# An edge-loop step of a graph attention layer: one VectorE product of 1024 columns instead of two of 512, and first-column additions at other places

## The chip, the cores and the metric

One core of one Trainium2 chip runs the kernel. The metric is the device time of one execution in microseconds (us), as the median of several runs. The engines are TensorE (PE in the profile; PEld is its weight load), VectorE (DVE), ScalarE (ACT), GpSimd (POOL) and SyncE (SP). Each works through its own queue in order; semaphores make one wait for another, or for its own earlier instruction.

## The reference

Relation-aware graph attention, a residual and a layer norm, in float32. N = 6250 nodes of 256 features, E = 100000 edges sorted by destination, 5 relations, 4 heads of 64.

```python
Q = (einsum('nc,rch->rnh', x, Wq) + bq[:, None, :]).reshape(R, N, HEADS, OUT)   # K, V alike
q_i = Q[edge_type, dst];  k_j = K[edge_type, src];  v_j = V[edge_type, src]
score = sum(q_i * k_j, axis=-1) * scale
seg = dst * R + edge_type
m = segment_max(score, seg);  e = exp(score - m[seg]);  s = segment_sum(e, seg)
alpha = e / s[seg]
out = segment_sum(v_j * alpha[..., None], dst).reshape(N, HD) + bias
x = layernorm(x + out, axis=-1)
```

## The kernel before

**Stages.** First the edges are sorted by segment on VectorE (a sorting network) while TensorE projects x to Q, K and V, which go to tables in HBM. Then comes the edge loop, which is what this document is about, and then a short stage that joins chunk borders, adds bias and x, and normalizes.

**The edge loop.** The edges stand in 831 tiles of 128, four tiles to a step, so 208 steps (`NSB`), and eight steps (`PERC`) make a chunk of 32 tiles, for which the softmax is worked out together. Every engine walks the same steps `s`, and later parts of a tile's work lag behind: payload by 13 steps (`AHEAD`), aggregation by 14 (`LAG`), first columns by 16. In step `s`:

- GpSimd (L486 and L504 are its gathers; L504 is the loop's) gathers K and V rows of 128 edges per indirect DMA, four a step, into a ring of 23 steps. Before a step's gathers it waits until TensorE has aggregated the tiles that lay there (`s_agg`, 18 steps back) and until VectorE has finished the product of five steps earlier (`s_mul`).
- SP (L558 to L569) loads the queries of the segments and the segment numbers (`bcr`), three steps ahead (`QS` = 3); it waits for `s_lift`.
- VectorE makes a turned one-hot matrix from the segment numbers (L1234, for step s+2).
- TensorE lifts the queries to edges with it: `lift(s + 1)`, four matmuls of 256 columns into the PSUM tile `qk` (`pairs`, two banks, L742). There is one such tile, so the lift of a step overwrites what the product of the step before reads.
- VectorE multiplies K by `qk` (`products`, L1245, in two halves of 512 columns, one bank each) and sums over 64 columns (`scores`, L1251).
- Once a chunk, over five steps, come the softmax parts: `weights_a` and `weights_b` on VectorE (scans L1255, L1256, L1261, L1262 and small operations), with transposes by TensorE (L689 to L717) and copies by ScalarE (L874 to L912). In `weights_a` five steps of eight have work for VectorE, three have none.
- Payload: ScalarE multiplies V by the weights for three tiles of four (L921), VectorE for one (L1312), or for three of four in the drain, the steps after the last product.
- VectorE makes the one-hot matrices of the destinations (L1303, four a step); TensorE aggregates with them (`aggregate`, L730, eight matmuls a step, in PSUM `sums`).
- ScalarE copies each tile's 128-column window into `acc` (L939) and the remaining columns of a step's four tiles into `cols` (L947). VectorE adds the first column of each tile into `acc` (`add_first`, L1330): 128 x 2 elements at an address read from a table (L1321 loads eight such addresses every second step). Neighbouring tiles may touch the same column, so each addition waits for the one before (`s_acc`).

The profile names SBUF tiles that are cut from one large one `region`, and counts a float32 matmul as two instructions, so a lift shows x8 and an aggregation x16.

**The order on VectorE** is written out by hand in the loop at the function's end:

```python
products(s, 0);  add_first(q - 2, 0, at)
products(s, 1);  add_first(q - 2, 1, at)
weights_a(s);    add_first(q - 2, 2, at)
scores(s);       payload(u);  turned_one_hot(s + 2)
add_first(q - 2, 3, at);      one_hot(q + 1);  ...;  weights_b(s)
```

TensorE's order is `lift(s + 1)`, `weights_a(s)`, `aggregate(s - 14)`, `weights_b(s)`. ScalarE's is: a window, a payload piece, and so on for four windows, then `cols` and the rest of the payload.

## Time and profile before

| | us |
|---|---|
| median of 3 runs | 2319.21 |
| lowest, highest | 2308.51, 2320.37 |
| span of the profiled execution, first to last instruction | 1977.2 |
| median above that span | 342.0 |
| busy in the span: TensorE, VectorE | 1614.3, 1597.6 |
| busy in the span: GpSimd, ScalarE | 1192.8, 1042.2 |

For the profiled execution the profile gives its span; its own time as a run is not among the three. The span starts at the first instruction that the profiler shows and ends with the last, so the runs' times are longer by what lies around it. Busy shares over the whole span mix stages with different limits. The edge loop runs from about 746 us (first gather) to 1830 us (last product), its drain to about 1894. A row of the timeline has the start, the duration, the engine, the line, the operation and, in brackets, how long the engine had been idle and what ended that. On VectorE an instruction's duration reaches past the start of the next one, so what it costs is read from start to start.

### The profile page before, as it was taken

How to read it: one execution, taken by the hardware profiler on the slowest of the kernel's cores; microseconds unless marked ns; L12 is line 12 of the kernel's file. 1: busy time of each engine (PE TensorE's matmuls, PEld its weight loads, DVE VectorE, ACT ScalarE, POOL GpSimd, SP SyncE). 2: the span in 40 equal slices, each digit the busy share in tenths (PEclk: the TensorE clock that was granted, in tenths of full speed). 3: DMA queues.
4: the chain of work that ended last, by engine and by line, in shares of the span. 5: the costliest groups of instructions: out<-in, count | busy, mean ns of one | idle time of the engine just before them, and what ended most of it. 6: DMA issues, size and time to landing. Idle time of an engine off the chain costs nothing.

```text
span 1977.2 us, 32984 instructions
## 1 busy us (share of the span) xinstructions
PE 1614.3 (82%) x7427; PEld 1118.3 (57%) x7427; DVE 1597.6 (81%) x4148; ACT 1042.2 (53%) x4032; POOL 1192.8 (60%) x1278
## 2 busy tenths in 40 slices
PE   5999889999999994777878877788788877778645
PEld 2455444444444443566667666676666666666634
DVE  7888897544443344799999999999999999999757
ACT  1333322210000000388888888888888888888625
POOL 2111114677777756777777777777777777776105
PEclk9999999999999997799999999999999999999778
DMA  8999999799999999999999999999999999998007
GB/s 223 276 257 265 244 253 247 244 342 364 362 363 363 364 348 312 336 337 328 331 332 318 334 338 327 331 324 333 330 328 326 324 336 338 325 333 287 25 14 226
DMA packets 349631, 592.55 MB, mean 300 GB/s; under 512 B 45391, under 2 KB 240157, under 8 KB 349434
## 3 DMA queue, kind: packets, MB, share of 16 engines
q0 software_dynamic: 90800, 293.85, 47.0%
q1 hardware_dynamic: 224310, 233.25, 35.8%
q10 hardware_dynamic: 34324, 63.35, 8.9%
q8 instruction: 60, 0.98, 0.2%
q14 instruction: 137, 1.12, 0.2%
HBM read 412.09 MB, written 140.94 MB: 280 GB/s over the span
## 4 chain that ended last, share of the span: by engine, by line
PE 29%; DVE 29%; issue 16%; DMA 11%; POOL 9%; DVEq 3%; ACT 2%; SPq 1%; ACTq 0%; POOLq 0%
PE sums L665 21%; POOL region L504 8%; DVE region L1303 6%; DVE region L1245 5%; PE pairs L742 5%; DMA region<-region 4%; DVE region L1037 4%; DVE region L1234 3%; DMA q_tab<-region 3%; DVE acc L1330 3%; PE sums L730 2%; DVEq L1321 2%; DVE region L1312 2%; DMA region<-in_x 1%; DMA region<-kv_tab,kvidx 1%
## 5 line engine op out<-in xcount | busy, mean ns | idle before, releaser
L504 POOL DMA_INDIRECT region<-kv_tab,kvidx x831 | 803.1, 966 | 289.1 <-issue 230.1
L665 PE MATMUL sums<-region,acc 128*128 128x512 f32 (+2 forms) x1568 | 664.9, 577 | 28.4 <-ACT acc L806 21.1
L921 ACT ACTIVATE region<-region 128x64 f32<-128x64 f32 x2392 | 662.5, 346 | 0.8
L742 PE MATMUL pairs<-region 128*128 128x256 f32 x1664 | 437.3, 408 | 197.2 <-DVE region L1245 180.2
L665 PEld LDWEIGHTS sums<-region,acc 128*128 128x128 f32 (+1 forms) x1568 | 292.7, 192 | 335.1 <-issue 289.5
L742 PEld LDWEIGHTS pairs<-region 128*128 128x128 f32 x1664 | 314.7, 199 | 268.8 <-issue 220.4
L730 PE MATMUL sums<-region 128*128 128x131 f32 x3328 | 429.9, 283 | 33.8 <-issue 23.3
L730 PEld LDWEIGHTS sums<-region 128*128 128x128 f32 x3328 | 411.6, 196 | 64.8 <-issue 47.5
L1211 DVE TENSOR_TENSOR region<-sums,region 128x512 f32<-128x512 f32 (+1 forms) x225 | 155.0, 691 | 234.4 <-PE sums L665 230.8
L939 ACT COPY acc<-sums 128x256 f32 x832 | 302.3, 363 | 57.3 <-PE sums L730 53.4
L486 POOL DMA_INDIRECT region<-q_tab,region x288 | 273.1, 948 | 91.0 <-issue 65.9
L1245 DVE TENSOR_TENSOR region<-region,pairs 128x512 f32<-128x512 f32 x416 | 277.4, 672 | 20.6 <-DMA region<-kv_tab,kvidx 19.9
L1251 DVE TENSOR_REDUCE region<-region 128x16 f32<-128x1024 f32 x208 | 252.4, 1214 | 0.9 <-issue 0.2
L898 ACT COPY region<-bank 128x128 f32<-128x128 f32 x26 | 6.9, 265 | 388.7 <-PE bank L709 387.8
L1303 DVE TENSOR_SCALAR region<-iota_f,nrel 128x131 f32<-128x131 f32 x832 | 203.9, 322 | 4.0 <-PE sums L730 3.9
L826 ACT COPY region<-sums 128x512 f32<-128x512 f32 (+1 forms) x167 | 86.3, 527 | 227.5 <-PE sums L665 106.5
L1037 DVE TENSOR_TENSOR region<-region 128x512 f32<-128x512 f32 x292 | 188.9, 688 | 5.1
L454 POOL DMA_DIRECT2D region<-region x49 | 43.2, 883 | 245.9 <-ACT region L826 245.9
L1330 DVE TENSOR_TENSOR acc<-acc,region 128x2 f32 x832 | 128.2, 154 | 20.4 <-ACT region L947 6.7
L1234 DVE TENSOR_SCALAR region<-region,part_f 128x512 f32<-128x512 bf16 x208 | 106.3, 511 | 8.5 <-DMA region<-rel_tab 8.5
L513 POOL TENSOR_TENSOR region<-region 128x256 f32<-128x256 f32 (+1 forms) x49 | 35.4, 731 | 112.4 <-DMA region<-in_x 111.8
L1312 DVE TENSOR_TENSOR region<-region 128x256 f32<-128x256 f32 x234 | 95.7, 418 | 1.1 <-ACT region L912 1.1
(239 smaller groups left out, 901.6 us busy)
## 6 DMA issues: line engine op xcount, KB each, us to landing
region<-q_seg SPq DMA_DIRECT2D x832, 128.0 KB
kv_tab<-region ACTq DMA_DIRECT2D x44, 1280.0 KB, 7.7
q_seg<-region SPq DMA_DIRECT2D x288, 128.0 KB, 5.5
region<-region POOLq DMA_DIRECT2D x48, 640.0 KB, 6.7
q_tab<-region SPq DMA_DIRECT2D x48, 640.0 KB, 5.9
region<-rel_tab SPq DMA_DIRECT2D x208, 128.0 KB
region<-kv_tab,kvidx POOLq DMA_INDIRECT x831
region<-in_x SPq DMA_DIRECT2D x96, 128.0 KB, 3.4
```

The costliest lines, as they stand in the source:

```text
L486: pool.indirect_dma_start(pq[:, j % PQ, :], None, q_tab, bass.IndirectOffsetOnAxis(ap=seg_list[:, j:j + 1], axis=0)).then_inc(s_pq[j % PQ] ...
L504: pool.indirect_dma_start(ring_row[:, a:a + 2 * C], None, kv_tab, bass.IndirectOffsetOnAxis(ap=kvidx[:, t:t + 1], axis=0)).then_inc(s_got[ ...
L665: done = nc.tensor.matmul(bank[o % 4][0:n, 0:w], acc[:, k, t * P:t * P + n], w_sb[:, k, :, :].rearrange("p u c -> p (u c)")[:, c0:c0 + w], ...
L730: done = nc.tensor.matmul(bank[i][:, h * W:(h + 1) * W], ring_v[:, i, spot(q), h * P:(h + 1) * P], oneh[:, q % 2, i, :], start=True, stop= ...
L742: done = nc.tensor.matmul(qk[:, i, :], oht[:, s % 2, i * P:(i + 1) * P], qring[:, s % QS, i, :], start=True, stop=True)
L921: done = nc.scalar.activation(ring_v[:, i, spot(q), h * D:(h + 1) * D], ring_v[:, i, spot(q), h * D:(h + 1) * D], ACT.Copy, scale=alT[:, h ...
L939: nc.scalar.copy(acc[:, :, bass.ds(at[(q % 2) * SB + i] + 1, P)], bank[i][:, 0:2 * W].rearrange("p (h n) -> p h n", h=2)[:, :, 0:P]).then_ ...
L1037: nc.vector.tensor_tensor(to[:, :, half, :], one, other_half, ALU.max if half else ALU.min).then_inc(s_sort, 1)
L1245: nc.vector.tensor_tensor(prod[:, two, :], ring_k[:, two, spot(s), :], qk[:, two, :], ALU.mult).then_inc(s_mul, 1)
L1251: nc.vector.tensor_reduce(sc[:, (s // PERC) % 2, :, g:g + SB].rearrange("p h g -> p g h"), prod.rearrange("p i (h d) -> p i h d", h=H), AX ...
L1303: done = nc.vector.tensor_scalar(oneh[:, q % 2, i, :], iota_f[:, 1:W + 1], nrel[:, t:t + 1], None, ALU.is_equal)
L1330: nc.vector.tensor_tensor(acc[:, :, bass.ds(col, 1)], acc[:, :, bass.ds(col, 1)], cols[:, q % CS, i, :, 2:3], ALU.add).then_inc(s_acc, 1)
```

## The change

The product of a step becomes one instruction of 1024 columns over both banks of `qk`. Semaphores follow: `s_mul` and `s_lift` count one a step where they counted two, TensorE's lift waits for the whole product of the step before and signals once, and GpSimd and SP wait for the new counts. On VectorE the order becomes product, addition 0, `weights_a`, payload, addition 1, scores, addition 2, turned one-hot, addition 3, one-hots, `weights_b`. Sizes, buffers and what is computed stay the same.

```diff
@@ GpSimd and SP
-                    pool.wait_ge(s_mul, 2 * (s - KL + 1))
+                    pool.wait_ge(s_mul, s - KL + 1)
...
-                    sp.wait_ge(s_lift, 2 * (s - QS + 1))
+                    sp.wait_ge(s_lift, s - QS + 1)
@@ TensorE, lift
-                for half in range(2):
-                    if s > 0:
-                        pe.wait_ge(s_mul, 2 * (s - 1) + half + 1)
-                    for i in (2 * half, 2 * half + 1):
-                        done = nc.tensor.matmul(qk[:, i, :], oht[:, s % 2, i * P:(i + 1) * P], qring[:, s % QS, i, :],
-                                                start=True, stop=True)
-                    done.then_inc(s_lift, 1)
+                if s > 0:
+                    pe.wait_ge(s_mul, s)
+                for i in range(SB):
+                    done = nc.tensor.matmul(qk[:, i, :], oht[:, s % 2, i * P:(i + 1) * P], qring[:, s % QS, i, :],
+                                            start=True, stop=True)
+                done.then_inc(s_lift, 1)
@@ VectorE, products
-                dve.wait_ge(s_lift, 2 * s + half + 1)
+                dve.wait_ge(s_lift, s + 1)
                 if s > 0:
                     dve.wait_ge(s_sc, s)
-                two = slice(2 * half, 2 * half + 2)
-                nc.vector.tensor_tensor(prod[:, two, :], ring_k[:, two, spot(s), :], qk[:, two, :], ALU.mult
-                                        ).then_inc(s_mul, 1)
+                nc.vector.tensor_tensor(prod[:], ring_k[:, :, spot(s), :], qk[:], ALU.mult).then_inc(s_mul, 1)
@@ VectorE, the loop
                 if s < NSB:
-                    products(s, 0)
+                    products(s)
                 if adds:
                     dve.wait_ge(s_cols, q - 1)
                     add_first(q - 2, 0, at)
-                if s < NSB:
-                    products(s, 1)
+                weights_a(s)
+                if 0 <= u < NSB:
+                    payload(u)
                 if adds:
                     add_first(q - 2, 1, at)
-                weights_a(s)
+                if s < NSB:
+                    scores(s)
                 if adds:
                     add_first(q - 2, 2, at)
-                if s < NSB:
-                    scores(s)
-                if 0 <= u < NSB:
-                    payload(u)
                 if s + 2 < NSB:
                     turned_one_hot(s + 2)
```

VectorE's queue in step 102, which has no softmax work, before. `ISA` is the address arithmetic of an addition and carries the addition's waits; TENSOR_REDUCE is `scores`, L1312 payload, L1234 the turned one-hot.

```order
L1245 TENSOR_TENSOR region<-region,pairs 128x512 [waits s_sc,s_lifted,s_got2]
L1330 ISA [waits s_acc,s_cols]
L1330 TENSOR_TENSOR acc<-acc,region 128x2
L1245 TENSOR_TENSOR region<-region,pairs 128x512 [waits s_sc,s_lifted]
L1330 ISA [waits s_acc]
L1330 TENSOR_TENSOR acc<-acc,region 128x2
L1330 ISA [waits s_acc]
L1330 TENSOR_TENSOR acc<-acc,region 128x2
L1251 TENSOR_REDUCE region<-region 128x4x4 [waits s_mul]
L1312 TENSOR_TENSOR region<-region 128x256 [waits s_alT]
L1234 TENSOR_SCALAR region<-region,part_f 128x512 [waits s_lifted,s_rel2]
```

The same step after the change, where the lines are L1242 (product), L1326 (addition), L1308 (payload), L1247 (scores) and L1233 (turned one-hot).

```order
L1242 TENSOR_TENSOR region<-region,pairs 128x1024 [waits s_sc,s_lifted,s_got2]
L1326 ISA [waits s_acc,s_cols]
L1326 TENSOR_TENSOR acc<-acc,region 128x2
L1308 TENSOR_TENSOR region<-region 128x256 [waits s_alT]
L1326 ISA [waits s_acc]
L1326 TENSOR_TENSOR acc<-acc,region 128x2
L1247 TENSOR_REDUCE region<-region 128x4x4 [waits s_mul]
L1326 ISA [waits s_acc]
L1326 TENSOR_TENSOR acc<-acc,region 128x2
L1233 TENSOR_SCALAR region<-region,part_f 128x512 [waits s_lifted,s_rel2]
L1326 ISA [waits s_acc]
```

The additions no longer stand side by side, payload stands ahead of the reduction, and one product stands where two were.

TensorE's queue in the same step before: the end of an aggregation, the lift of step 103 and the next aggregation's first matmuls.

```order
L730 MATMUL sums<-region 128x131 [waits s_pay_dve]
L730 MATMUL sums<-region 128x131
L742 MATMUL pairs<-region 128x256 [waits s_mul,s_oht,s_gotq1]
L742 MATMUL pairs<-region 128x256
L742 MATMUL pairs<-region 128x256 [waits s_mul]
L742 MATMUL pairs<-region 128x256
L730 MATMUL sums<-region 128x131 [waits s_pay,s_cols,s_oh]
L730 MATMUL sums<-region 128x131
```

The same place after the change, where the lift is L741:

```order
L730 MATMUL sums<-region 128x131 [waits s_pay_dve]
L730 MATMUL sums<-region 128x131
L741 MATMUL pairs<-region 128x256 [waits s_mul,s_oht,s_gotq1]
L741 MATMUL pairs<-region 128x256 x3
L730 MATMUL sums<-region 128x131 [waits s_pay,s_cols,s_oh]
L730 MATMUL sums<-region 128x131
```

The lift has one wait for a product instead of two; the matmuls stand in the same order.

## Rows read from the trace of the kernel before

**Rows 1.** Busy by stage: us, each engine, PE clock, DMA share, GB/s

```profile
746.70:868.20 121.50, 79.36 (x325) 60.75 (x326) 87.67 (x190) 38.96 (x159) 92.25 (x96) 0.78 0.98 335
868.20:1830.20 962.00, 760.31 (x4775) 658.06 (x4774) 945.92 (x2872) 812.83 (x3358) 710.82 (x735) 0.98 0.97 328
```

**Rows 2.** Groups, 868.2 to 1830.2 us; busy, mean ns | idle before, releasers

```profile
L504 POOL DMA_INDIRECT region<-kv_tab,kvidx x735 | 710.8, 967 | 241.8 <-issue 202.4 <-PE sums L730 34.2 <-DVE region L1245 5.2
...
L1245 DVE TENSOR_TENSOR region<-region,pairs 128x512 f32<-128x512 f32 x370 | 247.4, 672 | 0.0
...
L1255 DVE TENSOR_TENSOR_SCAN region<-XF,region 128x128 f32<-128x128 bf16 x46 | 20.2, 440 | 0.3 <-ACT region L878 0.3
```

**Rows 3.** Timeline of VectorE, products of steps 24 and 207

```profile
879.08 0.67 DVE L1245 TENSOR_TENSOR region<-region,pairs 128x512 f32<-128x512 f32 x1
...
1830.26 0.68 DVE L1245 TENSOR_TENSOR region<-region,pairs 128x512 f32<-128x512 f32 x1
```

**Rows 4.** Timeline of VectorE, step 102, without softmax work

```profile
1285.95 0.68 DVE L1245 TENSOR_TENSOR region<-region,pairs 128x512 f32<-128x512 f32 x1
1286.55 0.15 DVE L1330 TENSOR_TENSOR acc<-acc,region 128x2 f32 x1
1286.62 0.68 DVE L1245 TENSOR_TENSOR region<-region,pairs 128x512 f32<-128x512 f32 x1
1287.22 0.45 DVE L1330 TENSOR_TENSOR acc<-acc,region 128x2 f32 x2
1287.58 1.22 DVE L1251 TENSOR_REDUCE region<-region 128x16 f32<-128x1024 f32 x1
1288.71 0.41 DVE L1312 TENSOR_TENSOR region<-region 128x256 f32<-128x256 f32 x1
1289.04 0.48 DVE L1234 TENSOR_SCALAR region<-region,part_f 128x512 f32<-128x512 bf16 x1
1289.44 0.15 DVE L1330 TENSOR_TENSOR acc<-acc,region 128x2 f32 x1
...
1290.44 0.67 DVE L1245 TENSOR_TENSOR region<-region,pairs 128x512 f32<-128x512 f32 x1
```

**Rows 5.** Timeline of GpSimd and VectorE, loop start and gather 96

```profile
746.71 0.94 POOL L504 DMA_INDIRECT region<-kv_tab,kvidx  x1 [18.36 <-DVE region L1227]
...
756.94 0.69 DVE L1245 TENSOR_TENSOR region<-region,pairs 128x512 f32<-128x512 f32 x1 [0.78 <-DMA region<-kv_tab,kvidx]
...
868.23 0.97 POOL L504 DMA_INDIRECT region<-kv_tab,kvidx  x1 [0.30 <-issue]
```

**Rows 6.** Who waited for whom, 868.2 to 1830.2 us: total us, times, longest

```profile
PE pairs L742 <- DVE region L1245: 154.0, 155, 1.9
...
POOL region L504 <- PE sums L730: 34.2, 56, 2.6
```

**Rows 7.** Loop start, 746.7 to 868.2 us: GpSimd's group, a wait

```profile
L504 POOL DMA_INDIRECT region<-kv_tab,kvidx x96 | 92.2, 961 | 47.3 <-issue 27.7 <-DVE region L1227 18.4 <-PE sums L730 0.6
...
DVE region L1245 <- DMA region<-kv_tab,kvidx: 19.9, 11, 2.8
```

**Rows 8.** Timeline of three engines around the product of step 104

```profile
1291.26 1.97 PE L742 MATMUL pairs<-region 128*128 128x256 f32 x8 [0.72 <-DVE region L1245]
...
1293.07 1.96 PE L730 MATMUL sums<-region 128*128 128x131 f32 x16
...
1295.17 0.27 ACT L898 COPY region<-bank 128x128 f32<-128x128 f32 x1 [0.52 <-PE bank L709]
...
1295.08 0.68 DVE L1245 TENSOR_TENSOR region<-region,pairs 128x512 f32<-128x512 f32 x1
...
1296.64 0.42 DVE L1255 TENSOR_TENSOR_SCAN region<-PEN,region 128x128 f32<-128x128 bf16 x1
```

**Rows 9.** Timeline of TensorE and GpSimd at a half-clock spot

```profile
1320.78 3.14 PE L730 MATMUL sums<-region 128*128 128x131 f32 x16
...
1324.19 0.94 POOL L504 DMA_INDIRECT region<-kv_tab,kvidx  x1 [2.60 <-PE sums L730]
```

More of the change, by code:

```diff
@@ L569, in _ @@
                     sp.dma_start(qring[:, s % QS, i, :], q_seg[bass.ds(at[i], P), :]).then_inc(s_gotq[s % QS], 16)
-            sp.wait_ge(s_lift, 2 * NSB)
+            sp.wait_ge(s_lift, NSB)
             sp.dma_start(bias_sb[:], bias.rearrange("(o c) -> o c", o=1).broadcast_to([P, C])).then_inc(s_bias, 16)
@@ L1232, in turned_one_hot, with products @@
                 if s >= 2:
-                    dve.wait_ge(s_lift, 2 * (s - 1))
+                    dve.wait_ge(s_lift, s - 1)
                 nc.vector.tensor_scalar(oht[:, s % 2, :], bcr[:, s % QS, :], part_f[:, 0:1], None, ALU.is_equal
                                         ).then_inc(s_oht, 1)
-            def products(s, half):
-                if half == 0:
-                    dve.wait_ge(s_got[s % KL], gathered(s))
-                dve.wait_ge(s_lift, 2 * s + half + 1)
+            def products(s):
+                dve.wait_ge(s_got[s % KL], gathered(s))
+                dve.wait_ge(s_lift, s + 1)
                 if s > 0:
                     dve.wait_ge(s_sc, s)
-                two = slice(2 * half, 2 * half + 2)
-                nc.vector.tensor_tensor(prod[:, two, :], ring_k[:, two, spot(s), :], qk[:, two, :], ALU.mult
-                                        ).then_inc(s_mul, 1)
+                nc.vector.tensor_tensor(prod[:], ring_k[:, :, spot(s), :], qk[:], ALU.mult).then_inc(s_mul, 1)
             def scores(s):
-                dve.wait_ge(s_mul, 2 * s + 2)
+                dve.wait_ge(s_mul, s + 1)
                 g = SB * (s % PERC)
```

## The prediction

> **What bounds the kernel now.** Read first the busy time by stage [rows 1]. From 868.2 to 1830.2 us, half of the run, the edge loop goes its even way: VectorE is busy 945.9 of 962.0 us, while TensorE, ScalarE and GpSimd are at 79, 84 and 74%. The DMA share is 0.97 in the same row, so ask next whether VectorE waits for data. The groups of instructions say no: the products (L1245, 370 of them in this stretch) have 0.0 us of idle time before them, the scans that follow a copy by ScalarE (L1255 over XF) 0.3 us in all [rows 2]. VectorE sets the pace there.
>
> How long is a step? A product starts at 879.08 (step 24) and the last step's (207) at 1830.26 [rows 3]: 951.2 us for 183 steps, 5.20 a step, 41.6 for a round of eight. Steps differ by their softmax work: the first five of eight have some in `weights_a`, the last three (s mod 8 of 5 to 7) have none. [Rows 4] show one of those three, from 1285.95 to 1290.44, 4.49 us.
>
> Who stands just behind? GpSimd's 74% misleads. A gather takes 967 ns [rows 2], and the 0.30 us of "issue" before it [rows 5] belongs to it: 1.27 us each, 5.08 for the four of a step, against VectorE's 5.20. What it waits beyond that is 34.2 − 56×0.30 = 17 us for TensorE's sums [rows 6]. In the first 24 steps it waits for nobody: gather 0 starts at 746.71, gather 96 at 868.23 [rows 5], 1.266 us apart, and there VectorE waits for its gathers, 19.9 us in 11 waits [rows 7]. So two speeds lie close together: GpSimd at 5.06 to 5.08 us a step, VectorE at 5.20.
>
> **The change, part by part.**
>
> *One product of 1024 columns.* Durations overlap, so starts are compared. A 512-column product holds the engine 0.60 us (1285.95 to 1286.55, again 1286.62 to 1287.22), the reduction of 1024 columns 1.13 (1287.58 to 1288.71) [rows 4]. I take 1.13 for the new product, the nearest row in columns, though it reads SBUF alone: 2×0.60 − 1.13 = 0.07 saved a step. Bounds: 0.00, if two halves' cost just adds up, and 0.14, if the merged one saves twice that.
> By these rows the part of an instruction that doesn't grow with its columns is 0.60 − (1.13 − 0.60) = 0.07 us, though one operand lies in PSUM. The Trainium skill ("Perfetto Trace Analysis", Optimizing Scalar/DVE Operations) gives about 125 ns for VectorE on PSUM and 60 on SBUF. By its PSUM figure a step would save 0.125, as an estimate 0.055×183 = 10 us more than by the row; I go by the row.
>
> *The additions.* Behind a long operation one costs 0.07 us (1286.55 to 1286.62). In the three steps without softmax work the second and third stand back to back, and each waits for the one before: 0.36 for the pair (1287.22 to 1287.58) [rows 4], so 0.29 from one start to the next. Apart they cost 0.14: 0.22 saved in three steps of eight. In the other five they were apart already: nothing. The new places cover that 0.29: payload (1288.71 to 1289.04, 0.33), the reduction and the turned one-hot (1289.04 to 1289.44, 0.40) lie between.
>
> *Sum for VectorE.* 8×0.07 + 3×0.22 = 1.2 us a round, 41.6 to 40.4, or 5.05 a step. From step 24 to 207 are 22.9 rounds: 28 us (bounds 15 with a merged product at 1.20, 41 with 0.14 saved).
>
> *What cuts it off.* GpSimd issues the same 831 gathers. At the early pace the last starts at 746.71 + 830×1.266 = 1797.5, at the steady 1.27 at 1800.8. The first product came 10.2 us after the first gather's start [rows 5], so 6.4 after its fourth's (3×1.266 later), and the last product can't start before 1804 to 1807. VectorE alone would reach 1802. The later decides, with some friction where the two take turns; I take 1807, 23 us before 1830.26. The transfers keep up at that pace: in the first 24 steps they moved 335 GB/s, against 328 later [rows 1].
>
> *What TensorE loses.* The lift of step s+1 overwrites what product s reads, and now waits for all of it. Before, the half took 0.67 us and the lift began 0.15 behind it, 0.82 after the product's start (1290.44 to 1291.26) [rows 4, 8]. Now it begins at 0.67 + 0.53 + 0.15 = 1.35. It still ends at 1.35 + 1.97 = 3.3, before the next product even of a 4.2 us step. The aggregation behind it ended 4.59 after the product's start (1295.03) [rows 8], now at 5.12; the next lift can't begin before 4.2 + 1.35 = 5.55. TensorE's queue keeps 0.4 us in the shortest steps, so the later lift is costed at nothing. Its 154.0 us of waiting for L1245 [rows 6] is that slack, and stays about as long.
> Behind it on ScalarE: the scores' copy (L898) finished at 1295.44, 0.36 after the product of 1295.08, and its scan came 1.56 after [rows 8]. Now 0.36 + 0.53 + 0.29 (the shorter step) = 1.18, against a scan at 1.56 − 0.14 = 1.42: 0.24 left. Carries hang on VectorE's last scans of a step, not on the lift, and are needed 0.14 earlier. SP's loads wait for the whole lift as before, 0.5 us later with three steps, some 15 us, until use: nothing.
>
> *Payload before the reduction* moves work and adds none. Where a round of new weights begins it stands 1.2 us after the product's start. The weights' way is aggregation, transpose, copy: 5.12 − 5.2 + 2×0.27 is +0.5, with the durations of L898 in [rows 8] for both. It waits for nothing.
>
> *Start, sort, projection and normalization* are untouched. In the drain, the 16 steps after the last product, the additions 1 to 3 stand together where 0 to 2 did: nothing, give or take 3 us.
>
> **The number.** Span 1977.2 − 23 = 1954. The runs' median, 2319.21, is 342.0 above the span; that part has nothing of the change: 2319.2 − 23 = 2296 us, 1.0% less.
>
> **Rivals.**
>
> *The later lift eats half* (0.17), where TensorE's clock is halved. At 1320.78 an aggregation took 3.14 us instead of 1.96, and a gather then waited 2.60 us [rows 9]. With 0.53 us less slack such a spot could cost VectorE 0.8, and the scan's 0.24 is thin. For: TensorE waited for L1245 155 times. Against: 1 us each time, and the granted clock was 0.98 [rows 1]. Ten to fifteen spots at 0.8 give 8 to 12 us back: 2307.
>
> *The chain VectorE, TensorE, ScalarE, VectorE becomes the bound: slower* (0.05). Place: the waits of L1255 for the copies of scores and carries, twice for these, and payload's for new weights. If the copies come 0.75 us later than worked out (ScalarE does a window and a payload piece ahead of each), VectorE stands 0.5 us at four places a round: 2.0 against 1.2 won, and 0.8×22.9 = 18 us more, 2337. It decides once the four stalls sum to over 1.2. Against: 0.3 us in all is what L1255 over XF waited for the carries so far [rows 2]. The Trainium skill has a rule that speaks for it (same page, same section): where VectorE isn't saturated but causes bubbles on other engines, breaking up its instructions may let work finish sooner. The trace has the bubbles, TensorE's 154.0 us, but not the idle VectorE, which is busy 98%.
>
> *Transfers or GpSimd hold the old pace* (0.13). The DMA share is 0.97 already; if gathers land later when asked for faster, products wait, and a third is gained: 7 us, 2312. GpSimd itself is hardly slowed: its gathers took 961 ns beside a VectorE at 72% and 967 at 98% [rows 1, 2, 7], 5 us in all 831.
>
> *The change does nothing for VectorE* (0.05): the merged product takes 1.20 and other waits take the additions' place: 2319.
>
> **Chances.** Forecast 0.60 (2288 to 2303), half eaten 0.17, old pace 0.13, nothing 0.05, slower 0.05. A measurement of this kernel can tell about 0.5%, 11.6 us, from no change. Faster by more: 0.60 and most of the 0.17, 0.75; within: 0.20; slower: 0.05. The range goes from 2285 (VectorE's best bound, with gathers a little quicker) to 2314 (old pace), and leaves out the last two cases.
>
> **What would show it.** Right: 208 products that hold the engine 1.13 us; short steps of 4.2 us; waits of VectorE for gathers in the middle of the loop, where there are none; GpSimd's waits for TensorE's sums near 0.30 each; the last product at 1804 to 1810. Wrong: idle time before scans or payload that ends with ScalarE; short steps of 4.4; gathers above 1.28 us each.

## The result, and the profile after

| us | before | changed kernel | ratio, 95% interval |
|---|---|---|---|
| timed with the forecast on record | 2315.47 | 2340.86 | 1.0085 [1.0063, 1.0106] |
| again, session 4 | 2315.99 | 2330.36 | 1.0056 [1.0028, 1.0083] |
| again, session 6 | 1978.01 | 1973.39 | 0.9969 [0.9957, 0.9982] |
| forecast | 2319.2 | 2296 (2285 to 2314) | 0.990 |

The forecast was wrong in sign for the measurement it was made for. One sentence is needed to read everything below: the kernel before takes 2315 to 2335 us in five sessions and 1978 us in two (one chip showed both, and the executions of a session agree within 1%), and its profiled execution (span 1977.2) was of the second kind while the runs shown beside it were of the first. I call them late sessions (an engine starts late behind another's signal there, as shown below) and prompt sessions. The medians of the first row are of six executions of each kernel; the forecast started from the 2319.2 of three.

The span is the time within 2 us in both kinds of session: 2318.1 for a run of 2319.85 of the kernel before (late), 1974.6 for one of 1976.40 of `k3` below (prompt). So what stands ahead of the prediction, that the 342.0 us between median and span lie around the span, is wrong.

**Where the two kinds part.** Beside the prompt execution of the kernel before, the late one (`b0` below) is 148 us later at the first gather (894.9 against 746.7), loses 32 more up to product 24, 161 from there to product 207 (1111.9 against 951.2) and nothing behind it (147.1 against 146.9). Up to 380 us the two agree within 4 us; then ScalarE's casts behind TensorE's transposes come late in ten passes, one after the other, about 15 us in each, and that is the 148. One such cast in the late execution, and the same one in the prompt:

```profile
399.42 0.27 ACT L856 CAST XF<-pairs 128x129 bf16<-128x129 f32 x1 [12.65 <-remote]
383.52 0.27 ACT L856 CAST XF<-pairs 128x129 bf16<-128x129 f32 x1 [1.51 <-PE pairs L648]
```

In brackets, "remote" means that the profile ties the semaphore update that ended the wait to no instruction; "issue" means that it shows no such update just before the instruction.

The changed kernel's profile is of a late session (span 2339.8 for 2341.59 us). By stage, from the first gather to the product of step 24 and from there to step 207's, the changed kernel, with TensorE's clock, the share of the DMA engines and GB/s at the end:

```profile
core 0: us, PE busy (x) PEld busy (x) DVE busy (x) ACT busy (x) POOL busy (x), PEclk, DMA share, GB/s
900.00:1062.60 162.60, 87.42 (x372) 66.10 (x372) 95.74 (x199) 45.95 (x188) 100.35 (x104) 0.76 0.86 273
1062.60:2191.50 1128.90, 788.01 (x4716) 667.56 (x4717) 927.62 (x2658) 807.58 (x3323) 710.80 (x727) 0.95 0.87 276
```

The kernel before in a late session, the same two stages:

```profile
895.00:1059.40 164.40, 90.77 (x373) 68.36 (x373) 99.77 (x225) 46.53 (x190) 100.04 (x105) 0.75 0.86 272
1059.40:2171.40 1112.00, 794.47 (x4726) 673.58 (x4727) 947.81 (x2838) 808.83 (x3325) 698.62 (x727) 0.95 0.88 280
```

Against [rows 1] no engine works more, and none is near full: VectorE is busy 947.8 of 1112.0 us, 85%, where it was 98%. The change takes 20 us of work from it (927.6), and the stretch is 17 us longer. So the time went into waits, marked "remote" or "issue", ahead of operations whose partner had long ended. The DMA share is 0.87 or 0.88 where it was 0.97, so the transfers have more room than before.

What late signals look like: GpSimd's gathers in the kernel before, late session.

```profile
1516.04 0.95 POOL L504 DMA_INDIRECT region<-kv_tab,kvidx  x1 [0.30 <-issue]
1517.29 0.95 POOL L504 DMA_INDIRECT region<-kv_tab,kvidx  x1 [0.30 <-issue]
1518.54 1.00 POOL L504 DMA_INDIRECT region<-kv_tab,kvidx  x1 [0.30 <-issue]
1520.80 0.95 POOL L504 DMA_INDIRECT region<-kv_tab,kvidx  x1 [1.26 <-remote]
```

Three gathers start 1.25 us apart, and the first of the next step, the one that waits for semaphores, 2.26 behind. 3×1.25 + 2.26 = 6.0 us a step is the pace of the whole loop there (48.4 us for a round of eight steps, against 41.6 in [rows 3]). SP's issues show it too: five transfers of a step (one of L562, four of L569) in 4.36 us here (1516.05 to 1520.41), where the prompt execution needs 3.01:

```profile
1516.05 0.33 SPq L562 DMA_DIRECT2D region<-rel_tab  x1
1516.89 3.52 SPq L569 DMA_DIRECT2D region<-q_seg  x4
1521.51 0.33 SPq L562 DMA_DIRECT2D region<-rel_tab  x1
```

The same two lines of SP in the kernel before, prompt execution:

```profile
1288.78 0.33 SPq L562 DMA_DIRECT2D region<-rel_tab  x1
1289.62 2.17 SPq L569 DMA_DIRECT2D region<-q_seg  x4
```

**Where the loss is.** In these late executions a round takes 48.4 us with either kernel (median of the differences of every eighth product's start, steps 24 to 200: 48.45 before, 48.48 changed). But some rounds take over 1 us more, up to 51.2: two of 22 before (3.1 us more in sum), ten of 22 with the change (21.5 in sum), and ten again in session 4. The difference, 18.4 us, is what the stretch from product 24 to product 207 grew by, 16.4 (1111.9 to 1128.3), within 2. A long round of the changed kernel, its step with the first scans:

```profile
1262.88 1.21 DVE L1242 TENSOR_TENSOR region<-region,pairs 128x1024 f32<-128x1024 f32 x1
1264.38 1.90 PE L741 MATMUL pairs<-region 128*128 128x256 f32 x8
1267.73 0.27 ACT L897 COPY region<-bank 128x128 f32<-128x128 f32 x1 [3.25 <-remote]
1268.10 0.42 DVE L1251 TENSOR_TENSOR_SCAN region<-PEN,region 128x128 f32<-128x128 bf16 x1 [3.82 <-issue]
1269.11 0.38 PE L689 MATMUL bank<-ident,anyc 128*1 128x128 f32 x2
1273.51 0.57 ACT L873 COPY region<-bank 1x512 f32<-1x512 f32 x1 [3.68 <-remote]
1274.12 0.41 DVE L1257 TENSOR_TENSOR_SCAN region<-region 1x128 f32<-1x128 f32 x1 [2.29 <-ACT region L873]
1274.78 1.18 DVE L1242 TENSOR_TENSOR region<-region,pairs 128x1024 f32<-128x1024 f32 x1
```

And an ordinary one of the same kernel:

```profile
1410.69 1.21 DVE L1242 TENSOR_TENSOR region<-region,pairs 128x1024 f32<-128x1024 f32 x1
1415.56 0.27 ACT L897 COPY region<-bank 128x128 f32<-128x128 f32 x1 [3.26 <-remote]
1415.92 0.42 DVE L1251 TENSOR_TENSOR_SCAN region<-PEN,region 128x128 f32<-128x128 bf16 x1 [3.85 <-issue]
1416.94 0.38 PE L689 MATMUL bank<-ident,anyc 128*1 128x128 f32 x2
1417.53 0.57 ACT L873 COPY region<-bank 1x512 f32<-1x512 f32 x1
1420.17 1.18 DVE L1242 TENSOR_TENSOR region<-region,pairs 128x1024 f32<-128x1024 f32 x1
```

The two agree to 0.02 us up to TensorE's transposes of the softmax rows (L689, done 6.6 after the product's start). ScalarE's copy of them follows 4.0 us later in the long round and 0.2 in the ordinary one, though ScalarE was idle; VectorE waits 2.29 us for it in the long one, and the step takes 11.90 instead of 9.48. Counted over the loop by what ScalarE's row copy and VectorE's scan behind it waited for (us in total, times, longest), the changed kernel:

```profile
ACT region L873 <- remote: 41.0, 10, 5.7
DVE region L1257 <- ACT region L873: 28.2, 11, 4.4
```

In the kernel before the copy (L874 there) waited so twice, 9.4 us in all. Ten late copies, ten long rounds; two and two. They are the same rounds, one by one: in the changed kernel, the kernel before, `m1`, `o1`, `l1`, `p1`, `p2`, `v1` and `d1` every round with a row copy over 2.5 us late is a long one, and no other is. The first is long in all of them and the twentieth in all but `p1`, so which rounds are hit is not chance alone. In `p3` it holds for one of two. It is not so in `h1` and `h2`, which move these copies, nor with one query load a step: late copies in 14 rounds and 5 long ones in `d2`, 19 and 4 in `d3`, whose ordinary round is longer, 49.3 and 50.8 us.

### The profile page after: what moved, and what is told of

The parts are those of the page before. It is cut to its first block, busy times and chain, and to the rows that moved or that the text cites. A ratio compares the mean times of both kernels' runs of the same rounds, so it can differ in the third digit from the quotient of the medians.

```text
span 2339.8 us, 32569 instructions
## 1 busy us (share of the span) xinstructions
PE 1674.6 (72%) x7427; PEld 1140.4 (49%) x7427; DVE 1586.0 (68%) x3940; ACT 1044.8 (45%) x4032; POOL 1200.9 (51%) x1278
## 4 chain that ended last, share of the span: by engine, by line
PE 28%; issue 20%; POOL 20%; DVE 9%; another core or an unknown queue 8%; DMA 7%; ACT 4%; SPq 2%; DVEq 1%; ACTq 0%; POOLq 0%
POOL region L504 20%; PE sums L665 18%; PE sums L730 5%; PE pairs L741 3%; DMA region<-region 3%; DVE region L1036 3%; DMA q_tab<-region 2%; ACT region L920 2%; DVE region L1242 1%; DMA region<-in_x 1%; SPq L569 1%; DVE region L1299 1%; ACT acc L938 1%; DMA kv_tab<-region 1%
## 5 line engine op out<-in xcount | busy, mean ns | idle before, releaser
L665 PE MATMUL sums<-region,acc 128*128 128x512 f32 (+2 forms) x1568 | 683.2, 589 | 28.7 <-ACT acc L805 19.4
L741 PE MATMUL pairs<-region 128*128 128x256 f32 x1664 | 444.6, 413 | 201.1 <-DVE region L1242 125.1
L730 PE MATMUL sums<-region 128*128 128x131 f32 x3328 | 450.4, 291 | 146.8 <-issue 139.7
L730 PEld LDWEIGHTS sums<-region 128*128 128x128 f32 x3328 | 424.8, 202 | 200.3 <-issue 187.9
L665 PEld LDWEIGHTS sums<-region,acc 128*128 128x128 f32 (+1 forms) x1568 | 298.2, 196 | 342.0 <-issue 292.4
L741 PEld LDWEIGHTS pairs<-region 128*128 128x128 f32 x1664 | 322.4, 204 | 266.8 <-issue 222.0
L1242 DVE TENSOR_TENSOR region<-region,pairs 128x1024 f32<-128x1024 f32 x208 | 250.2, 1203 | 45.1 <-issue 19.7
L1247 DVE TENSOR_REDUCE region<-region 128x16 f32<-128x1024 f32 x208 | 252.1, 1212 | 0.3
L1299 DVE TENSOR_SCALAR region<-iota_f,nrel 128x131 f32<-128x131 f32 x832 | 197.2, 314 | 35.0 <-remote 30.2
L1326 DVE TENSOR_TENSOR acc<-acc,region 128x2 f32 x832 | 129.2, 155 | 11.5 <-ACT region L946 6.4
L1308 DVE TENSOR_TENSOR region<-region 128x256 f32<-128x256 f32 x234 | 95.0, 415 | 26.5 <-ACT region L911 26.5
L1233 DVE TENSOR_SCALAR region<-region,part_f 128x512 f32<-128x512 bf16 x208 | 105.1, 505 | 10.9 <-issue 7.7
```

The source lines that it names most:

```text
L665: done = nc.tensor.matmul(bank[o % 4][0:n, 0:w], acc[:, k, t * P:t * P + n], w_sb[:, k, :, :].rearrange("p u c -> p (u c)")[:, c0:c0 + w], ...
L730: done = nc.tensor.matmul(bank[i][:, h * W:(h + 1) * W], ring_v[:, i, spot(q), h * P:(h + 1) * P], oneh[:, q % 2, i, :], start=True, stop= ...
L741: done = nc.tensor.matmul(qk[:, i, :], oht[:, s % 2, i * P:(i + 1) * P], qring[:, s % QS, i, :], start=True, stop=True)
L1242: nc.vector.tensor_tensor(prod[:], ring_k[:, :, spot(s), :], qk[:], ALU.mult).then_inc(s_mul, 1)
L1247: nc.vector.tensor_reduce(sc[:, (s // PERC) % 2, :, g:g + SB].rearrange("p h g -> p g h"), prod.rearrange("p i (h d) -> p i h d", h=H), AX ...
L1299: done = nc.vector.tensor_scalar(oneh[:, q % 2, i, :], iota_f[:, 1:W + 1], nrel[:, t:t + 1], None, ALU.is_equal)
```

## The experiments

Eighteen further runs in six sessions, with 4 to 12 executions of each kernel (one of `b0`) and 19 to 28 of the kernel before beside them. The ratio is to the latter.

| kernel | session, before | ratio, 95% interval | round, long ones |
|---|---|---|---|
| b0_before_again | 1, 2317.48 | - | 48.4, 2 |
| m1_merge_only | 1 | 1.0038 [1.0019, 1.0057] | 48.4, 8 |
| o1_order_only | 1 | 1.0002 [0.9987, 1.0016] | 48.5, 3 |
| l1_late_lift | 2, 2334.15 | 1.0011 [1.0000, 1.0022] | 49.2, 2 |
| v1_half_reduction | 2 | 1.0016 [1.0003, 1.0028] | 49.3, 2 |
| h1_half_step_shift | 2 | 1.0103 [1.0084, 1.0122] | 49.3, 2 |
| h2_shift_and_change | 2 | 1.0243 [1.0221, 1.0264] | 51.0, 0 |
| p1_one_wait | 3, 2334.63 | 1.0003 [0.9989, 1.0017] | 49.1, 1 |
| p2_one_wait_change | 3 | 1.0008 [0.9996, 1.0019] | 49.2, 2 |
| p3_three_waits | 3 | 0.9994 [0.9980, 1.0008] | 49.2, 2 |
| a1_change_again | 4, 2315.99 | 1.0056 [1.0028, 1.0083] | 48.4, 10 |
| d1_narrow_loads | 4 | 1.0007 [0.9991, 1.0024] | 48.4, 2 |
| d2_one_load | 4 | 1.0053 [1.0033, 1.0074] | 49.3, 5 |
| d3_one_load_change | 4 | 1.0209 [1.0181, 1.0237] | 50.8, 4 |
| k1_ring_before | 5, 1978.19 | 1.0006 [0.9992, 1.0020] | 41.5, 0 |
| k2_ring_change | 5 | 0.9975 [0.9961, 0.9989] | 41.1, 4 |
| a2_change_third | 6, 1978.01 | 0.9969 [0.9957, 0.9982] | 41.4, 1 |
| k3_ring_again | 6 | 0.9999 [0.9988, 1.0010] | 41.5, 1 |

The last column has the median round of the profiled execution (from product starts, after step 24) and how many of its 22 rounds were over 1 us longer than that.

**The kernel before again, the two parts apart.** `b0`: no edit.

> The kernel before, unchanged, for a trace of an execution that takes as long as its timed runs (2308 to 2320 us). Theory A (late signals): the trace on which the prediction rested (span 1977.2 us) showed a quicker course than any timed run; in this one the span is 2300 to 2320, the loop's steps take about 5.9 us instead of 5.20, VectorE is busy some 88% of the loop and waits for scans' copies, and semaphore counts arrive in bunches about 0.7 us apart, as in the trace of the changed kernel. Rival B (the change itself brought the new waits): the span is near 1977 again, steps 5.20, VectorE busy 98%, and only the changed kernel shows such waits.

It came out as Theory A says, span 2318.1 for 2319.85 us. `m1` has the diff's product, lift and waits, with the additions where they were; `o1` keeps two products, back to back, with the new order behind them:

```diff
 # m1
-                    products(s, 0)
+                    products(s)
...
-                    products(s, 1)
 # o1
                     products(s, 0)
+                    products(s, 1)
...
-                    products(s, 1)
```

> One product of 1024 columns, but additions, payload and scores in the order of before. Theory A1 (the later lift costs): TensorE's lift starts about 0.5 us later in each step of a loop that hangs on signals between engines, so this part alone is slower than before by most of the measured 0.85%, 0.6 to 1.2% (2330 to 2343 us). Theory A2 (the new order costs): this part alone is the same or faster, 2295 to 2320.

> Two products of 512 columns, one behind the other, each with its own signal to TensorE, and the additions, payload and scores in the order of the change. Theory A1: same as before or faster by up to 0.6% (2300 to 2320 us), since the lift's first half starts as early as before. Theory A2 (payload ahead of the scores makes the scores late, and the softmax chain hangs on them): slower by 0.6 to 1.2%, 2330 to 2343.

In a late session the merged product alone costs 0.38%, between the ranges of its two theories, and the order alone nothing; together they cost 0.85% and 0.56%. ScalarE's row copy waited "remote" 8 times in `m1` and 3 times in `o1`, as many as there are long rounds in each. The loss comes with the merge. Whether the new order adds to it isn't shown: the interval of `m1` overlaps the one of session 4.

**Is it the late lift, or VectorE's pace?**

```diff
 # l1, on the kernel before
-                        pe.wait_ge(s_mul, 2 * (s - 1) + half + 1)
+                        pe.wait_ge(s_mul, 2 * s)
 # v1, on the kernel before
-    prod.rearrange("p i (h d) -> p i h d", h=H), AX.X, ALU.add)
+    prod.rearrange("p i (h d) -> p i h d", h=H)[:, :, :, 0:D // 2], AX.X, ALU.add)
```

> The kernel before with one edit: both halves of TensorE's lift wait for the second half of the product, so that the lift starts about 0.5 us later, as it does with the merged product; VectorE's own work and the number of its instructions stay. Theory A (the late lift is what costs: it pushes TensorE's turning of the softmax rows back, and more rounds of eight steps become long): 4 to 10 long rounds (over 49.9 us) of the 22 between steps 24 and 207 against 2 in the kernel before, ratio 1.002 to 1.006. Theory B (the merged product costs through VectorE itself, by its longer hold or by having fewer signals): as the kernel before, ratio 0.998 to 1.002, 1 to 3 long rounds.

> The kernel before with the scores' reduction over 512 of its 1024 columns (the second half of every head's products is left out of the scores), which takes 0.53 us a step from VectorE and moves no signal of the lift. Theory A (handovers between the engines set the length of a round, VectorE's load does not): the ordinary round stays at 48.0 to 48.5 us, at most 0.5% faster, ratio 0.995 to 1.001. Theory B (VectorE still sets the pace in the timed runs, as my prediction had it, with GpSimd's 5.08 us a step as the floor): 4.2 us less a round, ratio 0.955 to 0.965; where GpSimd cuts it off, 0.985 to 0.992.

`l1` came out as Theory B says: 0.11% with the interval touching 1.0000, and two long rounds. But its session has an ordinary round of 49.2 us, not 48.4, and the whole change with one wait less (`p2`) lost nothing on the same chip either. So `l1` shows that the late lift costs little there, and doesn't tell what it costs where the merge was measured. `v1` is plain. VectorE's work in the loop, from product 24 to 207:

```profile
1055.30:2183.80 1128.50, 827.02 (x4711) 704.31 (x4710) 851.91 (x2838) 806.55 (x3313) 701.63 (x727) 0.92 0.86 276
```

VectorE (third of the busy times) is at 851.9, 96 us less than in the kernel before, and the kernel is 0.16% slower, just above Theory A's range. In a late session VectorE does not set the pace.

**Is it the scores' handover?** In the late timelines above VectorE idles 3.8 us for the copy of the scores. `h1` swaps what `weights_a` and `weights_b` hold for ages 1 to 4, on all three engines; on VectorE:

```diff
 def weights_a(s):
-    if age == 1:  ...  scans(ends, S_sb, PEN, ...)
-    if age == 2:  ...  c(scans(full, S_sb, PEN, ...))
+    if age == 2:
+        carries(k, 0, peak)
...
 def weights_b(s):
-    if age == 1:
-        carries(k, 0, peak)
+    if age == 1:  ...  scans(ends, S_sb, PEN, ...)
+    if age == 2:  ...  c(scans(full, S_sb, PEN, ...))
...
```

> The kernel before with the softmax work of ages 1 to 4 moved by half a step on all three engines: VectorE does its scans at the end of a step and the carries near the start of the next, TensorE turns rows behind the aggregation and carries behind the lift, ScalarE's copies follow. The copy of the scores then has a whole step more until VectorE's first scan. Same instructions, same work. Theory A (a round waits for the handover of the scores TensorE to ScalarE to VectorE, 3.5 us a round in the first scan's idle time): the step with s mod 8 of 0 falls from 9.45 to 6.5 or less, the round from 48.4 to 43 to 46 us, ratio 0.95 to 0.985. Theory B (something else has a period of 48.4 us, and the wait before the first scan is only where it shows): the wait turns up at another place, the round stays at 48.0 to 48.8, ratio 0.997 to 1.005.

> The same half step shift on top of the changed kernel (merged product and spread additions). Theory A (the change loses because its later lift delays a handover on which a round waits): with a step more of slack the merged product no longer makes rounds long, so against the kernel before 0.945 to 0.985 and not slower than the shift alone by over 0.2%. Theory B: ratio 1.005 to 1.010, as the change without the shift.

Both came out slower than any of their theories had it, and Theory A fell clearly. The wait of the first scan went (step 9.45 in `b0` to 6.86), and the next step rose from 6.3 to 10.5: it now waits ahead of the scan of the rows.

```profile
  issue: 66.7, 27
  ACT region L874: 40.4, 23
```

These are the idle times of VectorE before L1261 in `h1` (us, times). Eased at this one place, the chain of handovers made the round no shorter. And the change on top costs 1.4% here, more than without the shift.

**Is it GpSimd's waits?** It stands 2.27 us at each step's start, 8×(3×1.25 + 2.27) = 48.2.

```diff
 # p1 (on before) and p2 (on the change)
-                if s >= KL:
+                elif s >= KL:
                     pool.wait_ge(s_mul, ...)
 # p3
                     pool.wait_ge(s_mul, 2 * (s - KL + 1))
+                    pool.wait_ge(s_lift, 2 * (s - KL + 1))
```

> The kernel before with one wait of GpSimd less: from step 18 on it waits for the aggregation alone ahead of a step's four gathers, since that stands behind the product it also waited for. In all timed kernels so far the first gather of a step starts 2.2 to 2.4 us after the last of the step before, while the others stand 1.25 us apart; with one wait (steps 5 to 17) it is mostly 1.25. Theory A (GpSimd's two waits cost it 1 us a step in ordinary executions, and its 6.05 us a step set the round of 48.4 us): the distance falls to 1.25 to 1.7, the round to 41 to 45 us, ratio 0.93 to 0.975. Theory B (it waits there for an aggregation that really ends late, GpSimd only follows): distance 2.1 to 2.4 as before, ratio 0.997 to 1.003.

> The changed kernel with the same wait of GpSimd left out. Theory A: with GpSimd's extra microsecond gone the VectorE savings of the change may count: ratio against the kernel before 0.925 to 0.975, and at most equal to the one wait kernel without the change. Theory B: 1.005 to 1.010, as the change alone.

> The kernel before with one more wait of GpSimd ahead of each step's gathers, for a lift that was over long before (the lift of the product it waits for already). Theory A (each wait of its own costs GpSimd some 1 us in ordinary executions): the distance rises by 0.7 to 1.0 us, the round to 54 to 57 us, ratio 1.04 to 1.09. Theory B (a wait that is satisfied costs it nothing): 0.998 to 1.002.

The number of waits costs nothing: the distance stayed at 2.2 to 2.4 in all three, and `p1` and `p3` came out as their Theory B says. `p2`, outside both of its ranges, is the change without a loss, 1.0008, and had two long rounds instead of ten. Whether that is the wait's doing isn't shown, since in sessions 2 and 3 the ordinary round was 49.2 us for other kernels as well, and the change itself was not run there.

**Is it the loads?**

```diff
 # d1, on the kernel before
-  sp.dma_start(qring[:, s % QS, i, :], q_seg[bass.ds(at[i], P), :])
+  sp.dma_start(qring[:, s % QS, i, 0:C // 4], q_seg[bass.ds(at[i], P), 0:C // 4])
 # d2 (before) and d3 (change)
-                for i in range(SB):
+                for i in range(1):
                     sp.dma_start(qring[:, s % QS, i, :], ...)
...
-  matmul(qk[:, i, :], oht[...], qring[:, s % QS, i, :], ...)
+  matmul(qk[:, i, :], oht[...], qring[:, s % QS, 0, :], ...)
```

> The changed kernel again, beside other kernels on one chip. Its loss of 0.85% either repeats (ratio 1.005 to 1.011), or it hangs on the chip: where the ordinary round is 49.2 us rather than 48.4, the later lift may fit, and the ratio is 0.999 to 1.003, as with the one wait kernel made from it (1.0008).

> The kernel before with SP's four query loads of a step at a quarter of their width (256 of 1024 bytes a row; the lift then uses what lay in the rest, so part of the scores is left out). Same number of transfers, packets and signals, 0.39 MB of 1.69 MB a step less. Theory A (the bytes of the DMA engines set 6.05 to 6.15 us a step): the round falls to 42 to 45 us, ratio 0.93 to 0.97. Theory B (handling of transfers and signals by number, not by bytes): 0.99 to 1.002. Theory C (neither): 0.998 to 1.002.

> The kernel before with one query load a step instead of four (all four tiles are lifted from the first one's rows, so three quarters of the queries are left out). SP issues two transfers a step instead of five. Theory A (bytes): ratio 0.93 to 0.97 as with the narrow loads. Theory B (number of transfers and their signals): the same here, 0.93 to 0.97, but not with the narrow loads. Theory C (a chain between VectorE, TensorE and ScalarE): 0.998 to 1.002 in both.

> The changed kernel with one query load a step. If the load side is what bounds the ordinary executions, VectorE or GpSimd bounds this one, and the change should bring what was forecast: 5 to 28 us less than the one load kernel without the change, the step with no softmax work at 4.2 us. If not, it is slower than that one by 0.1 to 1.0%.

In `d2` and `d3` TensorE's wait counts one load instead of four. `d1` moved 216 GB/s instead of 280 at a DMA share of 0.75, in the same time: the bytes are not it. `d2` with two transfers a step for five was slower, by 0.5%, which no theory had; the change on top of it cost 1.4% more (2361.82 against 2328.55), above the 0.1 to 1.0% expected. The loss of the change repeated (`a1`).

**Is it the slack of GpSimd's wait for the aggregation?**

```diff
-    KL = 5
+    KL = 4
```

> The kernel before with KL = 4 instead of 5, one number: a step's gathers then overwrite the slot whose aggregation ended one step earlier (and whose product ended one step later), so that GpSimd's wait for TensorE's aggregation has 6 us more. Until now that aggregation ends 0.3 to 3.5 us before the gather that needs it, and GpSimd stands 2.27 us from gather to gather there, 6.05 a step, 48.4 a round, whatever I did to VectorE, to SP's loads or to the number of its waits. Theory A (that wait, with its signal arriving up to 1 us or more late, sets the pace of the ordinary executions): the distance falls to 1.25 to 1.6, the round to 41 to 45 us, ratio 0.93 to 0.975. Theory B (the wait only shows a pace set by a chain among VectorE, TensorE and ScalarE): the round stays at 48.0 to 49.3, ratio 0.997 to 1.005.

> The changed kernel with KL = 4. Theory A: GpSimd's wait is off the path, VectorE's work counts, and the change gives 5 to 28 us against the ring's change alone. Theory B: slower than the ring's change alone by 0.5 to 1.1%, with 6 to 12 long rounds, as the change was against the kernel before.

> The kernel before with KL = 4 once more, since its first timing fell on the chip of the quick kind, where no engine waits long for the aggregation (1.0006 there). On a chip of the slow kind, Theory A (GpSimd's wait for the aggregation, whose signal comes late, sets 6.05 to 6.15 us a step): distance between gathers at a step's start 1.25 to 1.6 instead of 2.27, round 41 to 45 us, ratio 0.93 to 0.975. Theory B (a chain among the three compute engines sets the round): round 48.0 to 49.3, ratio 0.997 to 1.005. On the quick kind: 1.000 to 1.001 under both.

> The changed kernel a third time. Two kinds of chips have turned up: three on which the kernel before takes 2316 to 2334 us and signals arrive in bunches 0.7 us apart, and one on which it takes 1978 us, as in the profile that the forecast was made from. On a chip of the first kind: ratio 1.000 to 1.011, with 4 to 12 long rounds where the ordinary one is 48.4 us. On one of the second kind: VectorE saves in the short steps (4.2 us), GpSimd and the gathers stand close behind, 4 to 10 us less in all, ratio 0.995 to 0.998; the forecast's full 23 us would be 0.988.

My texts speak of two kinds of chips; that was wrong: the chip of session 4 (late) is that of session 6 (prompt). `k1` and `k3` both fell on prompt sessions, where the ring's number changes nothing, so the question they were made for stays open. But `a2` and `k2` show the change in sessions like that of the forecast's profile: 4.6 us less than the kernel before, and 7.1 less than the ring's change alone (1970.99 against 1978.13). The stages of `a2`, first gather to product 24 and on to 207, beside [rows 1]:

```profile
742.50:875.20 132.70, 82.91 (x389) 65.81 (x389) 96.23 (x201) 48.29 (x201) 101.00 (x105) 0.87 0.98 333
875.20:1820.90 945.70, 735.56 (x4704) 646.40 (x4705) 920.55 (x2654) 791.37 (x3314) 717.25 (x727) 0.99 0.97 330
```

Its groups from 868 to 1830 us, beside [rows 2]:

```profile
L504 POOL DMA_INDIRECT region<-kv_tab,kvidx x733 | 723.2, 987 | 223.4 <-issue 189.0 <-PE sums L730 23.5 <-DVE region L1242 11.0
L1242 DVE TENSOR_TENSOR region<-region,pairs 128x1024 f32<-128x1024 f32 x185 | 222.6, 1203 | 17.0 <-DMA region<-kv_tab,kvidx 16.6
L1251 DVE TENSOR_TENSOR_SCAN region<-XF,region 128x128 f32<-128x128 bf16 x46 | 20.6, 448 | 1.1 <-ACT region L877 0.9
```

A step without softmax work, beside [rows 4], and the product of the step after next:

```profile
1275.63 1.21 DVE L1242 TENSOR_TENSOR region<-region,pairs 128x1024 f32<-128x1024 f32 x1
1276.76 0.15 DVE L1326 TENSOR_TENSOR acc<-acc,region 128x2 f32 x1
1276.83 0.42 DVE L1308 TENSOR_TENSOR region<-region 128x256 f32<-128x256 f32 x1
1277.17 0.15 DVE L1326 TENSOR_TENSOR acc<-acc,region 128x2 f32 x1
1277.24 1.21 DVE L1247 TENSOR_REDUCE region<-region 128x16 f32<-128x1024 f32 x1
1278.37 0.15 DVE L1326 TENSOR_TENSOR acc<-acc,region 128x2 f32 x1
1279.92 1.21 DVE L1242 TENSOR_TENSOR region<-region,pairs 128x1024 f32<-128x1024 f32 x1
...
1289.76 1.22 DVE L1242 TENSOR_TENSOR region<-region,pairs 128x1024 f32<-128x1024 f32 x1 [1.12 <-DMA region<-kv_tab,kvidx]
```

And all gathers and all products of `a2`, first and last start (min, median, max in ns ahead of them):

```profile
L504 POOL DMA_INDIRECT region<-kv_tab,kvidx x831: 944/948/1649, 742.5 to 1812.6; - x167
L1242 DVE TENSOR_TENSOR region<-region,pairs x208: 1182/1206/1223, 754.0 to 1820.9; 128x1024 f32<-128x1024 f32 x104
```

VectorE does what was forecast: the product holds it 1.13 us (1275.63 to 1276.76), each addition 0.07, the step lasts 4.29 and others 4.15. Summed over the eight medians a round has 40.6 us of VectorE's steps, 41.5 before. The mean round is only 0.2 us shorter: the steps with s mod 8 of 7 have a median of 4.8 instead of 4.7 (mean 5.05), because products now wait for gathers, 16.6 us in 19 waits where there was none. GpSimd has no room left: its idle time is 223.4 us for 733 gathers, 0.305 each, where the 0.30 belongs to the gather; before it was 241.8 for 735, of which 21 us were waiting.

## Why the prediction was wrong, point by point

- **"The runs' median, 2319.21, is 342.0 above the span; that part has nothing of the change."** This is the step that failed. Under 2 us lie around the span; of the 342, 148 arise ahead of the first gather and 193 between it and the last product, where the change works (product 24 to 207 takes 1112 instead of 951 us). The profiled execution was of a prompt session, the runs of late ones, and which engine sets the pace is not the same in the two.
- **VectorE sets the pace** [rows 1, 2]: true in prompt sessions (97% busy in `a2`), false in late ones, where half a reduction less a step (`v1`) bought nothing. There the saving of 20 us was real work saved, and lost.
- **One product, 1.13 us**: right, in both kinds. The Trainium skill ("Perfetto Trace Analysis", Optimizing Scalar/DVE Operations) gives about 125 ns for VectorE on PSUM, which would be 0.125 saved a step, as an estimate. The trace does not agree: the starts give 0.07, as [rows 4] did.
- **The additions, 0.22 in three steps of eight**: right; steps 4.15 and 4.16 us in the median, forecast 4.2, and the round's sum 40.6, forecast 40.4.
- **GpSimd as the cap, last product at 1804 to 1807**: the mechanism was right, and it decided in prompt sessions; the terms were too small. Last product 1820.9. The last gather starts at 1812.6, not at 1797.5 to 1800.8: (1812.6 − 742.5)/830 = 1.289 us apart, not 1.266 to 1.27; its product 8.3 us behind it, not 6.4. That is the rival "Transfers or GpSimd hold the old pace", and its aside that "GpSimd itself is hardly slowed" is wrong: a gather took 967 ns in [rows 2] and 987 here. 0.020×831 = 17 us, most of what VectorE had won. Beside `k3`, of the same session with VectorE's old code (969 ns), it is 16 ns (all 831 gathers: 985), 13 us. The median gather is as long as before, 948 ns against 947; more of them take over 1 us, 180 of 726 instead of 119 (127 in `k3`). The DMA share stayed 0.97. In late session 1 gathers took 961 ns in `b0`, 971 in `m1` and 974 in `o1`, so they lengthen with either part; why is not shown.
- **Sum, prompt**: forecast 23 us, found 4.6 (1978.01 to 1973.39) between medians, 9.3 at the last product in the profiles, of which 4.2 already lay at the first gather, ahead of anything that the change touches.
- **The later lift at nothing**: nearly right in prompt sessions. It starts 1.35 us after the product's start, as worked out. TensorE's wait for products did not stay "about as long" but rose to 205.6 us (154.0 in [rows 6]), and ScalarE waits 91.5 us for the turned rows (63.1 before); VectorE's waits for ScalarE's copies stay small, 4.1 us (1.6 before). In late ones the merge costs 0.38%, and `l1`, the late lift without the merge, 0.11% in another session; that the lift is what the merge costs is not shown.
- **Rival "chain VectorE, TensorE, ScalarE, VectorE", 0.05, 2337 us**: by sign, size and place this is what was measured (2340.86): VectorE waits for ScalarE's copies. But its price came from ScalarE's work ahead of each copy; what delays them is the signal, TensorE's end to ScalarE's start, up to 6 us, in ten rounds of 22 and not in each. That the size came out is luck: the price was four stalls in every round. It got too small a chance because [rows 2] were taken for the runs. The Trainium skill ("Perfetto Trace Analysis", Optimizing Scalar/DVE Operations) says that breaking up instructions may let work finish sooner where VectorE isn't saturated but causes bubbles on other engines. `m1` agrees in sign: VectorE at 84%, one product instead of two, 0.38% slower.

**Open.** What sets 48.4 us in late sessions: less load on VectorE, the softmax work half a step later, another number of waits on GpSimd, and fewer bytes or loads by SP did not shorten it; GpSimd's wait for the aggregation (`k1`) wasn't reached there. What decides whether a row copy is late: the two rounds above are alike to 0.02 us before it. What makes a session late. Each execution on record has a span and a granted clock from the profiler, so none tells whether the recording itself has a part in it. No version was faster than the kernel before in late sessions, clear of the noise; in prompt ones the change (0.31%) and the change with the ring's number (0.25%) were, and which of them is the better isn't shown.

## What to carry to other kernels

Compare the profiled span with the runs' time before anything else: here they are 2 us apart where they belong to one execution, and a gap of 15% meant that rows and runs came from different conditions, so that no term could be carried over unchanged. An engine that is 98% busy in a profile sets the pace in that execution; halving a cost of it, as `v1` does, tells within one run whether it does so in the timed ones. And where two engines stand within 3% of one another, as here, a saving on the first is worth at most the distance to the second, and the second one's durations can move with the first one's order.

## What the hardware showed unexpectedly

- Signals can be late for a whole session: from TensorE's transpose to ScalarE's copy 0.04 us in the prompt execution, 2.6 (before) and 3.2 us (changed) for the scores' copy and up to 6 us for the rows' in late ones, and up to 16.8 us for the casts ahead of the loop. In the loop of `b0` the updates of semaphores stand in groups about 0.7 us apart, and the trace holds 8863 of them from product 24 to 207, where the prompt execution has 31043; behind the last product, where no time is lost, the two have 2293 and 2290. One in ten of SP's issues takes 0.68 us or more there, 0.33 in the prompt execution. The product's mean is the same, 1203 ns late and 1204 prompt.
- Less load did not make late sessions faster, and twice made them slower: one query load for four +0.5%, half a reduction +0.16%; a quarter of the loads' bytes changed nothing (1.0007 [0.9991, 1.0024]). TensorE's mean granted clock was 0.901 and 0.890 there, 0.906 in the kernel before and 0.875 in the slowest kernel (`h2`); whether the clock is cause or sign is open.
- A gather's mean duration moves with the order of VectorE's work beside it, at the same transfers: 961 ns before and 974 with the new order (`o1`, same session); 965 with half a reduction less (`v1`) and 993 with the softmax work shifted (`h1`, same session). VectorE's code isn't all of it: `l1`, where only TensorE's wait differs, has 971.
